# The 31-tap filter of a delta-rule attention layer, moved from VectorE to TensorE as Toeplitz blocks

## The reference, cut to what matters

```python
xn = _layernorm(x)
v = silu(_causal_dwconv(xn @ W_v, conv_w_v))          # q and k in the same way
delta_out = _delta_rule_chunkwise(q, k, v, beta)      # recurrence over chunks of 32 steps
vc = v.reshape(b, l, H * DV)
fir_s = _causal_dwconv(vc, fir_short_w)               # 3 taps for each channel
fir_l = _causal_dwconv(vc, fir_long_w)                # 31 taps for each channel
gate_in = concatenate([xn, fir_s, fir_l, delta_out], -1)
hid = gelu(gate_in @ W_fuse1 + b_fuse1)
logits = hid @ W_fuse2 + b_fuse2                      # gives p_ctx (3 weights) and p_val
o = p_ctx[0] * fir_s + p_ctx[1] * fir_l + p_ctx[2] * delta_out + p_val * v
attention = rmsnorm(o, norm_w) @ W_o
experts: top 2 of 8 for each token; y = swish-gated MLP of W1, W2, Wg, Wl, W3
out = x + attention + experts
```

## Time and profile before

| | us |
|---|---|
| median of 3 runs | 995.54 (989.79 to 998.58) |
| profiled execution, its own time | 992.98 |
| its span, first to last instruction | 991.2 |
| mean granted TensorE clock, share of full | 0.77 |
| busy in the span: PE / DVE / ACT / POOL | 648.1 / 809.9 / 294.7 / 472.4 |

### The profile page before, as it was taken

How to read it: one execution, slowest core, us unless ns; L and a number is a source line. 1 busy time by engine, 2 the same in 40 slices (tenths; PEclk the granted TensorE clock), 3 DMA queues, 4 the chain that set the end, 5 groups by cost and what they waited for, 6 DMA issues and landing times.

```text
span 991.2 us, 25096 instructions
## 1 busy us (share of the span) xinstructions
PE 648.1 (65%) x10300; PEld 488.7 (49%) x10300; DVE 809.9 (82%) x1554; ACT 294.7 (30%) x528; POOL 472.4 (48%) x489
## 2 busy tenths in 40 slices
PE   2759202654798765879488886888797972562552
PEld 2757202533565554656366565665575651441431
DVE  4468996789979996998869999899879988688841
ACT  2234121234333432333322523334333420120120
POOL 5224478787534373332732445225632455717414
PEclk9756555567899887997889987999979885575575
DMA  5888552315532325340722225422532115203201
GB/s 186 325 319 297 159 202 66 88 43 192 129 114 91 124 90 134 109 157 10 186 86 99 92 89 130 151 92 92 161 90 90 59 46 120 72 21 96 78 12 53
DMA packets 90417, 117.68 MB, mean 119 GB/s; under 512 B 57280, under 2 KB 62400, under 8 KB 86336
## 3 DMA queue, kind: packets, MB, share of 16 engines
q1 hardware_dynamic: 77360, 66.61, 22.3%
q0 software_dynamic: 10720, 47.68, 14.5%
q10 hardware_dynamic: 2224, 1.79, 0.6%
HBM read 74.64 MB, written 42.50 MB: 118 GB/s over the span
## 4 chain that ended last, share of the span: by engine, by line
DVE 39%; PE 25%; issue 18%; POOL 10%; ACT 3%; DMA 3%; SPq 2%; DVEq 0%; POOLq 0%; ACTq 0%
DVE fir_l L1416 8%; DVE solve_prod L1390 6%; PE ps_shared L1527 5%; DVE solve_T L1397 3%; PE ps_l L1523 3%; PE ps_g L1523 3%; DVE work L1497 3%; DVE acc L1322 2%; PE ps_shared L1663 2%; POOL xs_d L972 2%; POOL sumsq L931 2%; DVE work L1501 2%; DMA work<-expert_weights 2%; POOL ssq_o L1027 2%; PE ps_shared L1693 2%
## 5 line engine op out<-in xcount | busy, mean ns | idle before, releaser
L1416 DVE SCALAR_TENSOR_TENSOR fir_l<-v_act,late_sb,fir_l 128x512 f32<-128x512 f32 x240 | 196.7, 820 | 5.1
L1035 POOL TENSOR_TENSOR z<-work,z 128x512 fp32r<-128x512 f32 x46 | 70.1, 1525 | 182.1 <-ACT z L1198 181.9
L1390 DVE TENSOR_TENSOR solve_prod<-solve_T,solve_L 128x2 f32<-128x2 f32 (+30 forms) x248 | 120.7, 487 | 5.7 <-DMA solve_L<-system_d 0.7
L1397 DVE TENSOR_REDUCE solve_T<-solve_prod 128x1 f32<-128x2 f32 (+30 forms) x248 | 101.9, 411 | 8.3
L1523 PE MATMUL ps_x<-xr,w_up 128*128 128x512 f32 x276 | 91.2, 457 | 20.5 <-DVE work L1497 9.8
L1523 PE MATMUL ps_g<-z,w_mid 128*128 128x512 f32 x276 | 82.6, 439 | 6.3 <-DVE work L1501 6.2
L1523 PE MATMUL ps_l<-z,w_mid 128*128 128x512 f32 x276 | 84.1, 443 | 0.7 <-DVE work L1506 0.7
L1527 PE MATMUL ps_shared<-v_b,inverse 32*32 32x32 f32 x1024 | 16.2, 237 | 102.4 <-issue 98.8
L999 POOL DMA_INDIRECT w_mid<-y_d,slot_i x64 | 66.6, 1041 | 20.9 <-issue 18.3
L1523 PEld LDWEIGHTS ps_x<-xr,w_up 128*128 128x128 f32 x276 | 52.3, 209 | 41.7 <-DVE work L1497 14.8
L1322 DVE SCALAR_TENSOR_TENSOR acc<-pre,late_sb,acc 128x512 f32<-128x512 f32 x72 | 59.4, 826 | 15.2 <-ACT acc L1103 13.4
(11 more groups left out here) (236 smaller groups left out, 1492.1 us busy)
## 6 DMA issues: line engine op xcount, KB each, us to landing
mid_d<-w_mid SPq DMA_DIRECT2D x8, 1024.0 KB, 6.7
work<-expert_weights SPq DMA_DIRECT2D x16, 384.0 KB, 5.5
xs<-xs_d SPq DMA_DIRECT2D x23, 256.0 KB, 2.9
y_d<-work SPq DMA_DIRECT2D x23, 256.0 KB, 2.0
xs_d<-solve_L SPq DMA_DIRECT2D x11, 512.0 KB, 5.8
xa_d<-xr SPq DMA_DIRECT2D x8, 512.0 KB, 3.1
xa<-xa_d SPq DMA_DIRECT2D x8, 512.0 KB, 4.3
up_d<-w_up SPq DMA_DIRECT2D x8, 512.0 KB, 4.1
```

Source lines behind the costliest of these rows:

```text
L1035: pool.tensor_tensor(low[:, :], up1[i], high[:, :].bitcast(FP), ALU.subtract).then_inc(S["z_low"], 1)
L1390: seq.mark(dve.tensor_tensor(prod, solve_T[:, 0:k, 0:i + 1], over(solve_L[:, i, 0:i + 1].unsqueeze(1), P, k, i + 1), ALU.mult))
L1397: made = dve.tensor_reduce(solve_T[:, 0:k, i], prod, AX.X, ALU.add, negate=True)
L1416: made = dve.scalar_tensor_tensor(runs(dst), v_act[par][:, :, at:at + CHUNK], weights[:, i:i + 1], runs(dst), ALU.mult, ALU.add)
```

## The change

The long filter becomes products on TensorE. For each of the 32 channels e of a head two blocks of 32x32 taps (`taps`, built on the host, 1 MB, loaded once by a DMA on ScalarE's queue): one that takes the run's own 32 steps to its 32 outputs, and one that takes the 32 steps of the run before (chunk before, same sequence). The moving operand is `head_vs[rows, at:at + 16, e]`, one channel of 16 runs, whose elements lie 32 floats apart; the output goes into a PSUM bank at `[rows, :, e]`, 32 floats apart as well. That is 32 channels x 2 blocks x 4 heads = 256 products with 16 columns in a window. The step `fir_l` does them in 4 parts of 64; `fir_l_out` is one transpose on VectorE that turns the bank into the channel layout. The tile `head_vs` keeps v for two windows with 4 more runs in front, which GpSimd copies from the window before (in `v_act`). The short filter stays as it was (1 step on ScalarE, 2 on VectorE), and the halo of `v_act` shrinks from 30 steps to 2. Further edits: `delta_tok` goes (its data lies in `mix_part[1]` from the start), some masks and `beta_rows` share tiles with others, `load_mid` of the first two tiles gets waits of its own, and the numbers of `PULL` are other ones, which reorders every engine's list.

```diff
 def flow(name, w, i):
     if name == "fir":
-        return [[(DVE_, 0.9 if i >= K_SHORT else 1.8)]] if i else [[(ACT_, 1.4)]]
+        return [[(DVE_, 0.9)]] if i else [[(ACT_, 0.7)]]
...
+    "fir_l": [[(PE_, 1.9)]], "fir_l_out": [[(DVE_, 0.7)]],
...
-PULL = {"beta": -100, "beta_T": -300, "choose": -50, "combine": -50, "conv": 600, "conv0": 100, "count": 450,
+PULL = {"beta": 200, "choose": -200, "combine": 100, "conv": -300, "conv0": 350, "delta_T": 600, "delta_T_out": -50,
...
     def filters(w):
         yield need(("v_act", w, 0))
         if w >= 1:
+            yield need(("fir_s_T", w - 1, 0))
+        for k in range(K_SHORT):
+            yield "fir", w, k, None
+
+    def long_filters(w):
+        yield need(("v_T", w, 0))
+        if w >= 1:
             yield need(("fir_l_T", w - 1, 0))
-        for k in range(K_LONG):
-            yield "fir", w, k, None
+        bk = yield TAKE
+        for k in range(PARTS):
+            yield "fir_l", w, k, bk
+        yield "fir_l_out", w, 0, bk
+        leave(bk, "fir_l", w + 1)
...
-        yield need(("fir", w, K_LONG - 1))
+        yield need(("fir", w, K_SHORT - 1), ("fir_l_out", w, 0))
...
# GpSimd, v_act
                     if w:
                         pool.wait_ge(S["v_act"], w)
+                        pool.wait_ge(S["head"], 3 * w)
+                        pool.tensor_copy(head_vs[par][:, 0:SEQS, :], head_vs[1 - par][:, RUNS:, :])
...
# ScalarE, before its list
+            act.dma_start(taps[:].rearrange("p e s i -> p (e s i)"), taps_in).then_inc(S["in_taps"], 16)
...
# VectorE
+                elif name == "fir_l_out":
+                    dve.wait_ge(S["fir_l_ps"], w + 1)
+                    if w:
+                        dve.wait_ge(S["fir_l_T"], w)
+                        dve.wait_ge(S["fuse_ps"], 2 * w)
+                    dve.transpose(runs(fir_l), ps[:, :].rearrange("p (r e) -> p r e", e=HD)).then_inc(S["fir_l"], 1)
...
# TensorE
+                elif name == "fir_l":
+                    filtered = ps[:, :].rearrange("p (r e) -> p r e", e=HD)
...
+                    for e in range(HD // PARTS * i, HD // PARTS * (i + 1)):
+                        for last, at in enumerate((SEQS, 0)):
+                            for h in range(HEADS):
+                                rows = head_rows(h)
+                                made = pe.matmul(filtered[rows, :, e], taps[rows, e, last, :], head_vs[par][rows, at:at + RUNS, e],
+                                                 start=e == 0 and not last, stop=bool(last), tile_position=(HD * h, HD * h),
+                                                 skip_group_check=True)
```

133 lines of the change are left out of this document (73 added, 60 removed).

## The result

The changed kernel takes **1014.5 us** (median of 4 runs, 1011.6 to 1018.2) against 994.9 for the kernel before in the same rounds: a ratio of 1.020 with an interval of 1.0145 to 1.026, 2% slower. In a later group of runs, on another chip, the same pair gave 1.0125 (1.006 to 1.019). I had forecast 950, with 0.09 for slower. The profiled execution spans 1011.8 us.

A forecast was written before the change was run, and what follows sets the result against it. VectorE was taken to decide the middle stage, TensorE after the change; 230 + 552 + 164 = 946 us of span, + 1.8 outside it = 948 against the profiled 993, on the median 950 us; range 893 to 990.

The forecast's parts named there:

- the middle stage: From the experts' start to the last `times`: TensorE 491 us busy at 89% gives 552 us, against 571 before.
- Removed and added work: VectorE falls from 809.9 to some 619 us; TensorE gets 4096 records, 62 to 126 us in all.
- rival four: Filter products: elements 128 bytes apart make a record much dearer; at 40 ns the result is 1033; chance 0.1.
- Rival two: Filter products: a narrow product is no cheaper than a wide one, 27 ns a record; 985; chance 0.15.
- drain: TensorE at changes of tiling mode: none seen; if each of 8 a window cost 0.26 us, 17 us longer.
- Packets: TensorE's instructions come in packets of about 128 small records each 3.85 us: 15 ns in a burst, 30 in long runs.
- First stage: Up to where the experts begin: 238 - 5 - 6 + 3 = 230 us (224 to 240).
- the 1 MB load: First stage: the new load shares the DMA engines with the expert images, 0 to 5.5 us, taken as 3.
- Last stage: After the last `times`, windows 6 and 7: 12 + 57 + 34 + 61 = 164 us, against 182.
- `fetch`: Last stage, GpSimd's list: 8 DMAs at 0.95 us between the last mixing and its `rms`, + 8 us.
- Three: Middle stage: the experts' handovers between single PSUM banks held it, not VectorE; it stays 571, result 969; chance 0.15.
- My check: Whole span: 991 less the chain's 79 us on the filter, plus 15 for each of the two last windows' products, 942.

The follow-up runs named there:

- the run with few products: Kernel after, order unchanged, with 32 of the 256 filter products of each window, the others left out: 975.3 us, 0.977 of the kernel before.
- The run with one burst: Kernel after, the four parts of each window's filter products issued together where the first part stands: 1051.0 us, 1.053 of the kernel before.
- the run with few filter steps: Kernel before, order unchanged, with 3 of the 30 VectorE steps of the long filter in each window: 972.1 us, 0.973 of the kernel before.
- the old table: Kernel after with the order table PULL of the kernel before put back: 1022.4 us, 1.024 of the kernel before.
- the new table: The PULL of the kernel after; put on the kernel before, with after's waits before the first two load_mid: 1102.5 us, 1.106.
- the doubled products: Kernel after, order unchanged, each filter product issued twice into the same place: 1213.6 us, 1.160 of the kernel before, on the slower chip.
- the half-width steps: Kernel before, order unchanged, the experts' three VectorE steps per turn on half their columns: 1021.4 us against 1044.4, 0.977.
- The bf16 kernel in the order of after: Kernel after, order unchanged, filter products in bf16, one record instead of two: 1062.7 us, 1.018, on the slower chip; 984.9 us, 0.990, on another.

## Why the prediction was wrong

**The step that failed** is in the middle stage: "TensorE is now the engine that decides. The one that decided before reached 89%; I take the same: 491 / 0.89 = 552 us." TensorE's 491 was right to 2 us. But VectorE's 89% before was not the share of an engine that decides. Most of its filter steps filled gaps: without them the stage is 11 us shorter, not the 57 that my rule gives for it (TensorE's 457.3 / 0.89 = 514). And TensorE, which did decide, idled 118.6 us before and went on doing so: 109 after, where 552 left it 61. Had I added what TensorE is given to its idle time as it stood, the stage would have been 491 + 119 = 610, and my sum 230 + 610 + 164 = 1004, within 1% of the 1011.8 measured. Part of that would have been luck: 610 is 11.5 too long, and the other two stages are 19 too short. TensorE's own share before, 79%, would have given 620. I had even written that most steps "filled gaps between other steps", and then priced the stage as if they had not.

**Removed and added work.** VectorE 633.6 against 619, products 14.5 ns a record against 15, 59.4 us of the 62 to 126. The operands with elements 128 bytes apart took no longer than the 15 ns of the 32-column products (no run has them side by side), so rival four (slower, 1033) had the sign right and its mechanism wrong. Rival two fell with it: a narrow record is cheap, at 14.5 ns over 4096 records, which is the time from one to the next; each by itself lasts 200 ns, over its neighbours. The Trainium skill, page TensorEngine Tiling (Array Packing), section Instruction Overhead, has some 60 cycles for each matmul, by my estimate 25 ns at 2.4 GHz; as a price for each record in a row the measurement decides, and here it is 14.5. I had seen no drain at a change between small and wide products and put it at nothing, after naming 17 us for it. There is a price, about 0.1 us a change. In the run with few products six wide ones in a row take 1.39 us, from the first to the start of what follows, where that and what went before are wide too, and 1.59 between small ones; the same two values recur through the middle stage of this and of the other traces:

```profile
254.70 1.55 PE L1541 MATMUL ps_l<-z,w_mid 128*128 128x512 f32 x6
256.09 0.86 PE L1541 MATMUL ps_x<-xr,w_up 128*128 128x512 f32 x3
...
306.87 1.67 PE L1541 MATMUL ps_g<-z,w_mid 128*128 128x512 f32 x6
308.46 0.32 PE L1702 MATMUL ps_shared<-head_vs,taps 32*32 32x16 f32 x16
```

At eight changes a window that is an estimated 4 us in the middle stage, as much as TensorE is busier there beside the products' own 33.4.

**Packets.** The reading was right (114 packets; 128 records each 3.5 to 3.7 us in a burst, where I had 3.85), and the order of after had mostly dealt with it: the parts are spread, and the stops at the products are 9.0 us in the middle, where I had 5. The run with one burst shows that it would have cost 39 us not to.

**First stage**, 230 forecast, 243.4 measured. "The 256 products of window 0 fall where TensorE has nothing else" was wrong. TensorE stands 22 us at them for VectorE's transpose, which costs nothing by itself (it is 21.8 without most of them too), but the burst with its stops, from 127 to 146 us, stands ahead of and between the products of the next projection (L1541), which end at 147.2 us, and at 135.3 with few products. GpSimd waits for what ScalarE makes of them between two of its scatters, 5.1 us, and not at all with few:

```profile
143.68 0.22 POOL L871 COPY pre<-pre 128x36 f32<-128x36 f32 x1 [5.12 <-ACT pre L1115]
```

Without most of the products the stage is 235.5. The last scatter starts at 218.1 us, or at 211.8 in that run; before 220.1. And the filter's steps ahead of the scatter were worth 2.5 us (238.0 to 235.5 with few steps), not 5. The 3 us that I gave to the 1 MB load can't be seen in these runs: the one with few products has the load too and its first stage is as short as that of the run with few filter steps, which has not; but their orders differ, so this shows no more than that it isn't large.

**Last stage**, 164 forecast, 169.9 measured, 182.2 before. I had VectorE 83% busy there until window 7 starts; by the earlier trace rows it is 86.7 of 107.7 us, 81%, which changes nothing in the sum. The `fetch` between the last mixing and its `rms` is there, and TensorE waits 21.0 us for the last mixed block in place of 11.2; I had 8 for it. VectorE has the sums for `rms` ready at 980.4, and GpSimd takes them up (L1044) only behind its eight DMAs, of which the first and the last are shown:

```profile
978.24 1.00 POOL L1020 DMA_INDIRECT w_mid<-y_d,slot_i  x1
...
987.05 0.94 POOL L1020 DMA_INDIRECT w_mid<-y_d,slot_i  x1 [0.30 <-issue]
988.06 0.21 POOL L1044 TENSOR_SCALAR ssq_o<-ssq_o 128x16 f32<-128x16 f32 x1
```

**The rivals.** Three was nearest: VectorE was not what held the middle stage. But it let the stage stay at 571, as if the products were free. They come on top, because TensorE is in the chain too. The account in measured terms: the steps' removal -27 (972.1), the products with the old table +50 (1022.4; of these some are stops for packets, and the planner's steps change too), the new table -4 to -11 by the ratios, after at +13 to +20. My check "991 less the 79 us that the chain spent on the filter" failed for the same reason as the sum: shares of the chain tell what was passed, not what would be saved.

## What to carry to other kernels

Before work is moved from the engine with the highest share to the next one, take it out of the old kernel with the order kept, and look at the gain: here 177 us of busy time were worth 27, and the products that replace them cost 39 to 50. In this kernel, whose engines each work off one list, the middle stage went with TensorE's busy time, and its many short waits stayed about as they stood; an addition to its list cost 0.7 to 0.85 of its own time (12 us for 17, 39 for 48, 50 for 59), though the engine looked idle for a fifth of the stage, and more where instruction packets had to be waited for. If a filter like this goes to TensorE, its records must be few (bf16, one for each product: 23 us) and spread between large products (39 us), and then the order has to be searched again for the new kernel (16 us here, where the same search made the kernel before slower by 8).

## What the runs showed that I had not expected

The kernels of one group (with the doubled products and the half-width steps) ran on a chip where the kernel before took 1044 us in place of 995 to 999. The traces from it show stretches of about ten us in which TensorE's small products come in handfuls, the stops far shorter and more frequent than one in each 126 records; between such stretches bursts of 128 run as elsewhere. Here in the kernel before with half-width steps:

```profile
864.19 0.30 PE L1527 MATMUL ps_shared<-u_adj,masked 32*32 32x32 f32 x6
864.87 0.34 PE L1527 MATMUL ps_shared<-u_adj,masked 32*32 32x32 f32 x4 [0.37 <-issue]
865.59 0.34 PE L1527 MATMUL ps_shared<-u_adj,masked 32*32 32x32 f32 x5 [0.39 <-issue]
866.36 0.33 PE L1527 MATMUL ps_shared<-u_adj,masked 32*32 32x32 f32 x4 [0.43 <-issue]
```

Five records each 0.75 us are 150 ns a record, ten times the price in a burst. In such stretches the instructions seem to come more slowly; what makes them do so, and whether it explains the whole 4.5%, wasn't tested. The bf16 kernel in the order of after stood at 1.018 there and 0.990 on another chip, so even a ratio to the kernel before in the same rounds did not carry from chip to chip; only kernels of one group should be set side by side.

TensorE's granted clock in the middle stage was 0.90 in the kernel before, with its own table and with the new one, and 0.81 to 0.88 in all the others, those with less work for TensorE too. With the filter's steps few and nothing else changed it was 0.88. TensorE was busy 5 us more there for the same list, which may be this clock; what lowers it was not tested.
